# Moving loads, the place of Pool's sum, and the low parts of h at the seams of a staged two-layer kernel

## The chip, the cores and the metric

The kernel runs on one core of one Trainium2 chip. The metric is the device time of one execution in microseconds, taken as the median of several runs. Engines are named as in the profile: PE (TensorE matmul, PEld its weight loads), DVE (VectorE), ACT (ScalarE), POOL or Pool (GpSimd), SP (SyncE, which here issues the loads).

## The reference

x has shape (B, T, S) = (1024, 24, 1024), W1 (1024, 24), W2 (1024, 1024), all float32. The output is (1024, 1024).

```
h = jax.nn.sigmoid(jnp.einsum('bts,st->bs', x, W1) + b1)
return h @ W2.T + b2
```

So every h[b, s] is a sum over 24 values x[b, t, s] with the weights W1[s, t], and then h meets W2 in a plain matrix product. x is 100 MB and is read once.

## The kernel before, in words

**Stages.** The rows b are in 8 blocks j of 128, the columns s in 8 chunks c of 128. A stage takes four blocks j (512 rows) and two to four chunks. There are five, numbered 0 to 4, in `STAGES` (L19 to L25), each as (first block, first chunk, number of chunks, number of t that Pool takes, places, fate). Stages 0 and 1 are the first 512 rows with chunks 0 to 3 and 4 to 7, stages 2, 3 and 4 the other 512 rows with chunks 0 to 2, 3 to 5 and 6 to 7. "The last seam" is the one between stages 3 and 4.

**Two ways for x.** In each stage the t below `pools[i]` (4 or 6) go to Pool, the others to PE and DVE.
- PE's way: the tile of one t (an *item*: 512 rows by all columns of the stage) is loaded into one of 5 slots of `ring` (L201). For each chunk PE turns it (four 128x128 transposes into one of 6 banks `xbank`, L232), and DVE adds it, weighed, into `acc` (L354; the first t of a stage starts `acc`, L348). One chunk of one t is a *unit*, of kind "x".
- Pool's way: the tile of one t is loaded in two halves of 256 rows (*parts*, numbered m through the whole kernel) into 6 slots of `nat` (L195). Pool multiplies a part by the row of W1 (`weigh`, L485) and adds the sum of the t before (`add_sum`, L495). The sum over Pool's t is then turned by PE like an x tile and added without a weight (L352): these are the units of kind "n".

**Order of units.** `units[i]` (L50 to L56) lists the units of a stage: x of all t but the last two, then the n units, then x of t = 22 and 23. PE and DVE both walk through that list, and item_end, sum_turned and chunk_end are worked out from it. In stage 4 (two chunks, six t of Pool's) units 0 to 31 are t = 6 to 21, 32 and 33 are n, 34 and 35 are t = 22, 36 and 37 are t = 23.

**Order of loads.** SP issues everything in one order written out in the tables. At place `at` of a stage, just ahead of the item of t = pools[i] + at, it issues one part if `at` is in the places. The parts run two ahead of the stages: with 10, 12, 12, 12 and 10 places the last two of each stage's places carry parts of the next stage. Parts 44 to 55 are stage 4's; 44 and 45 are issued at places 15 and 17 of stage 3. An item waits until PE has turned the item five before it (L200); a part waits until the sum has passed on from its slot (part m on the sum of part m-4, L191) or, behind a stage's end, until PE has turned the sum (L193).

**h and the products.** When a chunk of a stage is complete, ACT takes the sigmoid (L431) and casts it to `h_hi` (L456); `h_lo` is h - h_hi. Stages 0 to 3 have h_lo from Pool: `low_parts(i - 1)` (L497 to L501) runs behind the third part of stage i. The product of a stage is done by PE during the next stage, between the units, by `product_step` (L264, matmuls at L301): h_hi times w_hi and w_lo, and h_lo times w_hi. `steps_due` (L160) says how many steps are due after each unit. For the first two outputs the steps with h_lo come behind those with h_hi of both. Outputs go through two banks `pbank`; ACT copies them to `y` (L443) or DVE adds them to `y` (L371, `add_out`), and PE waits for that before it uses a bank again. In stage 4, `REST` = 12 of the steps are held back until all its units are turned (L318 to L320).

**The tail.** ACT's sigmoid of stage 4 waits until all products of stage 3 are summed (L450), DVE makes h_hi and h_lo in 128x128 pieces (L387, L389), PE multiplies into eight banks (L332), DVE adds to y (L371), SP stores (L211).

Of the kernel before, what the change touches and what calls it, by code (L numbers as in the profile page):

```python
# [5 lines left out]
F32 = mybir.dt.float32  # L6
F32R = mybir.dt.float32r
ALU = mybir.AluOpType
# [7 lines left out]

STAGES = (  # L19
    (0, 0, 4, 4, (2, 3, 5, 7, 9, 11, 13, 15, 17, 18), "keep"),  # L20
    (0, 4, 4, 6, (0, 2, 3, 5, 6, 8, 9, 11, 12, 14, 15, 17), "last"),
    (4, 0, 3, 6, (0, 2, 3, 5, 6, 8, 9, 11, 12, 14, 15, 17), "keep"),
    (4, 3, 3, 6, (0, 2, 3, 5, 6, 8, 9, 11, 12, 14, 15, 17), "add"),
    (4, 6, 2, 6, (0, 2, 3, 5, 6, 8, 9, 11, 12, 13), "last"),
)  # L25


def rec_kernel(nc, x, W1, b1, W2, b2, out):
    B, T, S = x.shape
# [3 lines left out]
    OH = O // BANK  # L33
    NS = len(STAGES)
    LAST = NS - 1
# [7 lines left out]

    chunks = [s[2] for s in STAGES]
    pools = [s[3] for s in STAGES]
    fate = [s[5] for s in STAGES]
    NK0, NK = pools[0], max(pools)
# [2 lines left out]

    units = []
    for i in range(NS):
        order = [("x", t, c) for t in range(pools[i], T - 2) for c in range(chunks[i])]
        order += [("n", 0, c) for c in range(chunks[i])]
        order += [("x", t, c) for t in range(T - 2, T) for c in range(chunks[i])]
        units.append(order)  # L56
    first_unit = [sum(len(o) for o in units[:i]) for i in range(NS)]
    UNITS = sum(len(o) for o in units)
    first_h = [sum(chunks[:i]) for i in range(NS)]
# [11 lines left out]
    parts = [(i, k, f) for i in range(NS) for k in range(pools[i]) for f in range(2)]  # L71
# [18 lines left out]
    with ExitStack() as ctx:  # L90
# [12 lines left out]
        h = sb("h", [P, CMAX, BANK])  # L103
        h_hi = sb("h_hi", [P, CMAX, BANK], F32R)
        h_lo = sb("h_lo", [P, CMAX, BANK], F32R)
# [32 lines left out]
        h_hi_ready = sem("h_hi_ready")  # L138
        h_lo_ready = sem("h_lo_ready")
# [42 lines left out]
        def _(sp):  # L182
            sp.dma_start(w1[:, :].rearrange("p (c t) -> p c t", t=T),
                         W1.rearrange("(c p) t -> p c t", p=P)).then_inc(w1_loaded, 16)
            m = 0
            for i, (j0, c0, n, _, places, _) in enumerate(STAGES):
                for at in range(T - pools[i]):
                    if at in places:
# [3 lines left out]
                        elif m >= NATS:  # L192
                            sp.wait_ge(unit_turned, sum_turned(parts[m - NATS][0]))  # L193
                        sj, sc, sn = STAGES[s][0] + HALF * f, STAGES[s][1], STAGES[s][2]
                        sp.dma_start(nat[:, m % NATS, :, :sn * P],  # L195
# [141 lines left out]
        @block.vector  # L337
        def _(dve):
            def add_unit(i, v):
                u = first_unit[i] + v  # L340
                kind, t, c = units[i][v]
                bank, total = xbank[u % XBANKS][:, :], acc[:, c, :]
                weight = w1[:, bass.ds((STAGES[i][1] + c) * T + t, 1)]
                dve.wait_ge(unit_turned, u + 1)
                if v < chunks[i]:
                    if i > 0 and c < chunks[i - 1]:
                        dve.wait_ge(h_ready, first_h[i - 1] + c + 1)
                    nc.vector.tensor_scalar(total, bank, weight, None, ALU.mult).then_inc(unit_added, 1)  # L348
                    return
                dve.wait_ge(unit_added, u - chunks[i] + 1)  # L350
                if kind == "n":
                    nc.vector.tensor_tensor(total, bank, total, ALU.add).then_inc(unit_added, 1)  # L352
                else:
                    nc.vector.scalar_tensor_tensor(out=total, in0=bank, scalar=weight, in1=total,  # L354
                                                   op0=ALU.mult, op1=ALU.add).then_inc(unit_added, 1)

            def split_w2(m):
                n, c = divmod(m, SC)
                cols = slice(n * BANK, (n + 1) * BANK)
                dve.wait_ge(w_hi_ready, m + 1)  # L360
                nc.vector.tensor_tensor(w_lo[:, c, cols], pbank[m % 2][:, :], w_hi[:, c, cols].bitcast(F32),  # L361
                                        ALU.subtract).then_inc(w_lo_ready, 1)

            def add_out(i, n, bank):

                j, cols = out_half(n)
                dve.wait_ge(out_summed, OUTS * i + n + 1)
                dve.wait_ge(part_kept, kept_at[i])
                if i > 0 and fate[i - 1] == "add":
                    dve.wait_ge(y_added, added_at[i - 1] + n + 1)  # L370
                nc.vector.tensor_tensor(y[:, j, cols], bank[:, :], y[:, j, cols], ALU.add).then_inc(y_added, 1)  # L371

            dve.wait_ge(w1_loaded, 16)
            for i in range(NS):
                for v in range(len(units[i])):
                    add_unit(i, v)
                    if i == 0 and v - 2 in W2S:
                        split_w2(W2S[v - 2])
                    if i > 0 and fate[i - 1] != "keep" and v >= 2:
                        for n in range(outs_due(i, v - 2), outs_due(i, v - 1)):  # L380
                            add_out(i - 1, n, pbank[n % 2])

            for c in range(chunks[LAST]):
                for j in range(JT):
                    rows = slice(j * P, (j + 1) * P)
                    dve.wait_ge(h_ready, first_h[LAST] + c * JT + j + 1)
                    nc.vector.tensor_copy(h_hi[:, c, rows], h[:, c, rows]).then_inc(tail_hi, 1)  # L387
                    dve.wait_ge(tail_hi, c * JT + j + 1)
                    nc.vector.tensor_tensor(h_lo[:, c, rows], h[:, c, rows], h_hi[:, c, rows].bitcast(F32),  # L389
                                            ALU.subtract).then_inc(tail_lo, 1)  # L390
            for n in range(outs_due(LAST, len(units[LAST]) - 2), OUTS):
                add_out(LAST - 1, n, pbank[n % 2])
            for n in range(OUTS):
                add_out(LAST, n, xbank[(UNITS + n) % XBANKS] if n < XBANKS else pbank[n - XBANKS])
# [66 lines left out]
        @block.gpsimd  # L461
        def _(pool):
            nc.gpsimd.memset(ident[:, :], 0.0).then_inc(ident_zeroed, 1)
            pool.wait_ge(ident_zeroed, 1)
            nc.gpsimd.affine_select(out=ident[:, :], in_=ident[:, :], compare_op=ALU.not_equal, fill=1.0, base=0,
                                    pattern=[[-1, P]], channel_multiplier=1).then_inc(ident_ready, 1)
            nc.gpsimd.memset(b2x[:, :].bitcast(F32), 0.0).then_inc(b2_zeroed, 1)
            nc.gpsimd.memset(ones[:, :].bitcast(F32), 1.0).then_inc(ones_ready, 1)
            pool.wait_ge(ones_ready, 1)
            pool.wait_ge(b2_zeroed, 1)  # L470
            pool.wait_ge(b2_rounded, 2)
            low = b2x[32:33, :].rearrange("a (h n) -> a h n", n=BANK)
            nc.gpsimd.tensor_tensor(low, h[32:33, 0:OH, :], low.bitcast(F32), ALU.subtract).then_inc(b2_ready, 1)
            pool.wait_ge(b2_ready, 1)

            def weigh(m):

                i, k, f = parts[m]
                _, c0, n, _, _, _ = STAGES[i]
                row = w1all[:, k, c0 * P:(c0 + n) * P].unsqueeze(1).to_broadcast([P, HALF, n * P])  # L480
                slot = nat[:, m % NATS, :, :n * P]
                pool.wait_ge(nat_loaded[m % NATS], 16 * (m // NATS + 1))
                if k == 0 and f == 0 and i < 3:
                    pool.wait_ge(set_kept, (EARLY, EARLY + NK, SETN)[i])
                nc.gpsimd.tensor_tensor(slot, slot, row, ALU.mult).then_inc(nat_weighed, 1)  # L485

            def add_sum(m):

                i, k, _ = parts[m]
                n = STAGES[i][2]  # L490
                slot = nat[:, m % NATS, :, :n * P]
                pool.wait_ge(nat_weighed, m + 1)
                if k > 1:
                    pool.wait_ge(nat_added, sums_made(m - 2))
                nc.gpsimd.tensor_tensor(slot, slot, nat[:, (m - 2) % NATS, :, :n * P], ALU.add).then_inc(nat_added, 1)  # L495

            def low_parts(i):  # L497
                for c in range(chunks[i]):
                    pool.wait_ge(h_hi_ready, first_h[i] + c + 1)
                    nc.gpsimd.tensor_tensor(h_lo[:, c, :], h[:, c, :], h_hi[:, c, :].bitcast(F32),  # L500
                                            ALU.subtract).then_inc(h_lo_ready, 1)  # L501

            for m, (i, k, f) in enumerate(parts):
                weigh(m)
                if k > 0:
                    add_sum(m)
                if i > 0 and k == 1 and f == 0:
                    low_parts(i - 1)


_INS = ["r_x", "L0_rec_W1", "L0_rec_b1", "L0_rec_W2", "L0_rec_b2"]
# [18 lines left out]
```

## Time and profile before

| what | value |
|---|---|
| median of 3 runs | 311.82 us (311.63 to 311.99) |
| the profiled execution | 311.89 us, its span 310.1 us |
| mean granted TensorE clock | 0.982 |
| PE busy | 257.8 us, 83% of the span |
| PE weight loads | 220.0 us, 71% |
| DVE busy | 246.4 us, 79% |
| POOL busy | 215.2 us, 69% |
| ACT busy | 50.9 us, 16% |
| DMA | 109.48 MB, of which 104.97 MB read |
| chain that ended last | PE 51%, DMA 31%, DVE 7%, issue 5%, ACT 3% |

The span runs from the first to the last instruction of the profiled execution; 1.8 us of its time lie around it. All times below are us from the start of the span. Starts and ends of matmuls in a timeline are modelled and overlap by a fraction of a microsecond; the chain cuts them where the next begins. A wait is put down to the engine or DMA that released it last.

### The profile page before, as it was taken

The page shows a single profiled execution, that of the slowest core. Times are in us where ns is not written, and L with a number is a line of the kernel's source. Part 1 is how long each engine was busy: PE and PEld are TensorE (multiplying, and loading weights), DVE is VectorE, ACT ScalarE, POOL GpSimd, SP SyncE. Part 2 cuts the span into 40 slices and gives each one's busy share as a digit, 9 for nine tenths or more (in the row PEclk, how much of TensorE's full clock was granted, in tenths as well). Part 3 has the DMA queues.
Part 4 walks back from the last instruction along what each step waited for, and adds up shares of the span by engine and source line. Part 5 has one row for each costly group of instructions (what it writes and reads, how often), then busy time and mean ns, then how long its engine had stood idle before and what let it go on. Part 6 is the DMA issues. An engine that isn't in the chain of part 4 may idle for free.

```text
span 310.1 us, 4779 instructions
## 1 busy us (share of the span) xinstructions
PE 257.8 (83%) x1761; PEld 220.0 (71%) x1761; DVE 246.4 (79%) x368; ACT 50.9 (16%) x85; POOL 215.2 (69%) x125
## 2 busy tenths in 40 slices
PE   0947678648888999999579999937999988999894
PEld 0846677647766888889468887835888885888783
DVE  0729899829998978889977987877878898798865
ACT  4211223203253100100420000040101104000120
POOL 3119676626379999995799977479988848999000
PEclk9979999959999999999999999999999999999999
DMA  7999999999999999999999999999999999999007
GB/s 223 398 390 385 387 385 386 402 387 388 385 387 384 387 386 388 386 385 384 373 374 374 385 381 381 381 385 373 373 373 373 370 359 340 339 349 332 29 2 272
DMA packets 67675, 109.48 MB, mean 353 GB/s; under 512 B 3642, under 2 KB 40514, under 8 KB 67652
## 3 DMA queue, kind: packets, MB, share of 16 engines
q1 hardware_dynamic: 67056, 107.06, 96.8%
q10 hardware_dynamic: 596, 2.11, 1.7%
q8 instruction: 14, 0.23, 0.3%
q14 instruction: 9, 0.07, 0.1%
HBM read 104.97 MB, written 4.19 MB: 352 GB/s over the span
## 4 chain that ended last, share of the span: by engine, by line
PE 51%; DMA 31%; DVE 7%; issue 5%; ACT 3%; SPq 1%; DVEq 0%; ACTq 0%
DMA ring<-in_r_x 31%; PE xbank L232 25%; PE pbank L301 20%; DVE acc L354 4%; PE xbank L332 3%; ACT h L431 2%; DVE w_lo L361 2%; ACT h_hi L456 1%; PE pbank L291 1%; PE pbank L332 1%; PE pbank L261 0%; DVE acc L352 0%; ACT L431 0%; SPq L195 0%; SPq L201 0%
## 5 line engine op out<-in xcount | busy, mean ns | idle before, releaser
L354 DVE SCALAR_TENSOR_TENSOR acc<-xbank,w,acc 128x512 f32<-128x512 f32 x280 | 200.0, 746 | 41.1 <-PE xbank L232 35.6
L232 PE MATMUL xbank<-ident,ring 128*128 128x128 f32 x1184 | 171.5, 279 | 44.2 <-DMA ring<-in_r_x 36.0
L232 PEld LDWEIGHTS xbank<-ident,ring 128*128 128x128 f32 x1184 | 142.2, 144 | 75.7 <-issue 27.9
L485 POOL TENSOR_TENSOR nat<-nat,w1all 128x768 f32<-128x768 f32 (+2 forms) x56 | 107.2, 1916 | 60.6 <-DMA nat<-in_r_x 47.1
L495 POOL TENSOR_TENSOR nat<-nat 128x768 f32<-128x768 f32 (+2 forms) x46 | 87.8, 1908 | 3.6
L301 PE MATMUL pbank<-w_hi,h_hi 128*128 128x512 f32 x112 | 48.2, 431 | 0.3 <-ACT h_hi L456 0.2
L301 PE MATMUL pbank<-w_lo,h_hi 128*128 128x512 f32 x112 | 48.3, 432 | 0.0
L301 PE MATMUL pbank<-w_hi,h_lo 128*128 128x512 f32 x112 | 40.5, 431 | 0.0
L431 ACT ACTIVATE h<-acc,b1col 128x512 f32<-128x512 f32 (+1 forms) x22 | 12.5, 599 | 96.1 <-DVE acc L354 64.0
L443 ACT COPY y<-pbank 128x512 f32<-128x512 f32 x16 | 9.4, 587 | 79.4 <-PE pbank L301 79.4
L301 PEld LDWEIGHTS pbank<-w_hi,h_hi 128*128 128x128 f32 x112 | 21.3, 191 | 1.4 <-ACT h_hi L456 1.0
L348 DVE TENSOR_SCALAR acc<-xbank,w 128x512 f32<-128x512 f32 x16 | 11.7, 746 | 13.1 <-PE xbank L232 9.2
L301 PEld LDWEIGHTS pbank<-w_lo,h_hi 128*128 128x128 f32 x112 | 21.3, 191 | 0.6
L500 POOL TENSOR_TENSOR h_lo<-h,h_hi 128x512 fp32r<-128x512 f32 x14 | 17.7, 1282 | 2.4 <-ACT h_hi L456 2.4
L301 PEld LDWEIGHTS pbank<-w_hi,h_lo 128*128 128x128 f32 x112 | 18.4, 191 | 0.5
L413 ACT CAST w_hi<-pbank 128x512 fp32r<-128x512 f32 x16 | 9.4, 587 | 39.3 <-PE pbank L261 39.3
L371 DVE TENSOR_TENSOR y<-pbank,y 128x512 f32<-128x512 f32 x18 | 12.2, 683 | 3.0 <-PE pbank L301 3.0
L261 PE MATMUL pbank<-ident,y 128*128 128x128 f32 x64 | 10.3, 285 | 1.0 <-DVE w_lo L361 1.0
L361 DVE TENSOR_TENSOR w_lo<-pbank,w_hi 128x512 fp32r<-128x512 f32 x16 | 10.8, 678 | 0.0
L352 DVE TENSOR_TENSOR acc<-xbank,acc 128x512 f32<-128x512 f32 x16 | 10.0, 679 | 0.0
L408 ACT COPY w1all<-pbank 128x512 f32<-128x512 f32 x12 | 7.0, 587 | 18.3 <-PE pbank L250 18.3
L250 PE MATMUL pbank<-ident,w 128*128 128x128 f32 x48 | 7.7, 286 | 1.5 <-DVE w_lo L361 1.5
(37 smaller groups left out, 93.1 us busy)
## 6 DMA issues: line engine op xcount, KB each, us to landing
ring<-in_r_x SPq DMA_DIRECT2D x38, 1024.0 KB, 13.4
ring<-in_r_x SPq DMA_DIRECT2D x36, 768.0 KB, 11.1
nat<-in_r_x SPq DMA_DIRECT2D x20, 512.0 KB, 13.1
nat<-in_r_x SPq DMA_DIRECT2D x24, 384.0 KB, 11.5
ring<-in_r_x SPq DMA_DIRECT2D x18, 512.0 KB, 7.8
y<-in_L_rec_W SPq DMA_DIRECT2D x2, 2048.0 KB, 14.9
nat<-in_r_x SPq DMA_DIRECT2D x12, 256.0 KB, 8.7
out_y<-y ACTq DMA_DIRECT2D x4, 512.0 KB, 6.6
```

Of the source, the lines that this page charges most:

```text
L232: mm = pe.transpose(xbank[u % XBANKS][:, j * P:(j + 1) * P], tile, ident[:, :])
L261: mm = pe.transpose(pbank[m % 2][:, j * P:(j + 1) * P], y[:, j, c * P:(c + 1) * P], ident[:, :])
L301: mm = pe.matmul(pbank[n % 2][:, :], a[:, c, rows], w[:, STAGES[i][1] + c, cols], start=r == 0, stop=r == per - 1)
L332: mm = pe.matmul(bank[:, :], a[:, c, j * P:(j + 1) * P], w[:, STAGES[LAST][1] + c, cols], start=c == 0 and k == 0, stop=c == chunks[LAST] ...
L348: nc.vector.tensor_scalar(total, bank, weight, None, ALU.mult).then_inc(unit_added, 1)
L354: nc.vector.scalar_tensor_tensor(out=total, in0=bank, scalar=weight, in1=total, op0=ALU.mult, op1=ALU.add).then_inc(unit_added, 1)
L361: nc.vector.tensor_tensor(w_lo[:, c, cols], pbank[m % 2][:, :], w_hi[:, c, cols].bitcast(F32), ALU.subtract).then_inc(w_lo_ready, 1)
L371: nc.vector.tensor_tensor(y[:, j, cols], bank[:, :], y[:, j, cols], ALU.add).then_inc(y_added, 1)
L431: nc.scalar.activation(h[:, c, rows], acc[:, c, rows], ACT.Sigmoid, bias=b1col[:, bass.ds(STAGES[i][1] + c, 1)]).then_inc(h_ready, 1)
L485: nc.gpsimd.tensor_tensor(slot, slot, row, ALU.mult).then_inc(nat_weighed, 1)
L495: nc.gpsimd.tensor_tensor(slot, slot, nat[:, (m - 2) % NATS, :, :n * P], ALU.add).then_inc(nat_added, 1)
L500: nc.gpsimd.tensor_tensor(h_lo[:, c, :], h[:, c, :], h_hi[:, c, :].bitcast(F32), ALU.subtract).then_inc(h_lo_ready, 1)
```

## The change

It does four things.

1. Stage 3 has 10 places instead of 12 (15 and 17 are dropped), stage 4 has 12 instead of 10 (1 to 6 and 8 to 13). Parts 44 and 45 are so issued at places 1 and 2 of stage 4, part 46 at place 3, the last one still at place 13. The number of loads and their sizes stay.
2. In the last stage all x units come first and the n units last: 32, 33 are t = 22, 34, 35 are t = 23, 36, 37 are n.
3. Pool's `low_parts` is gone.
4. DVE makes the low parts of stages 0 to 3 with the same operation: chunk c of stage i-1 behind unit chunks[i] + 2c of stage i.

```diff
@@ -16,12 +16,13 @@
 
 
 
+
 STAGES = (
     (0, 0, 4, 4, (2, 3, 5, 7, 9, 11, 13, 15, 17, 18), "keep"),
     (0, 4, 4, 6, (0, 2, 3, 5, 6, 8, 9, 11, 12, 14, 15, 17), "last"),
     (4, 0, 3, 6, (0, 2, 3, 5, 6, 8, 9, 11, 12, 14, 15, 17), "keep"),
-    (4, 3, 3, 6, (0, 2, 3, 5, 6, 8, 9, 11, 12, 14, 15, 17), "add"),
-    (4, 6, 2, 6, (0, 2, 3, 5, 6, 8, 9, 11, 12, 13), "last"),
+    (4, 3, 3, 6, (0, 2, 3, 5, 6, 8, 9, 11, 12, 14), "add"),
+    (4, 6, 2, 6, (1, 2, 3, 4, 5, 6, 8, 9, 10, 11, 12, 13), "last"),
 )
 
 
@@ -50,9 +51,10 @@
 
     units = []
     for i in range(NS):
-        order = [("x", t, c) for t in range(pools[i], T - 2) for c in range(chunks[i])]
+        ahead = T - 2 if i < LAST else T
+        order = [("x", t, c) for t in range(pools[i], ahead) for c in range(chunks[i])]
         order += [("n", 0, c) for c in range(chunks[i])]
-        order += [("x", t, c) for t in range(T - 2, T) for c in range(chunks[i])]
+        order += [("x", t, c) for t in range(ahead, T) for c in range(chunks[i])]
         units.append(order)
     first_unit = [sum(len(o) for o in units[:i]) for i in range(NS)]
     UNITS = sum(len(o) for o in units)
@@ -361,6 +363,11 @@
                 nc.vector.tensor_tensor(w_lo[:, c, cols], pbank[m % 2][:, :], w_hi[:, c, cols].bitcast(F32),
                                         ALU.subtract).then_inc(w_lo_ready, 1)
 
+            def low_part(i, c):
+                dve.wait_ge(h_hi_ready, first_h[i] + c + 1)
+                nc.vector.tensor_tensor(h_lo[:, c, :], h[:, c, :], h_hi[:, c, :].bitcast(F32),
+                                        ALU.subtract).then_inc(h_lo_ready, 1)
+
             def add_out(i, n, bank):
 
                 j, cols = out_half(n)
@@ -376,6 +383,10 @@
                     add_unit(i, v)
                     if i == 0 and v - 2 in W2S:
                         split_w2(W2S[v - 2])
+
+                    c, odd = divmod(v - chunks[i], 2)
+                    if i > 0 and 0 <= c < chunks[i - 1] and odd == 0:
+                        low_part(i - 1, c)
                     if i > 0 and fate[i - 1] != "keep" and v >= 2:
                         for n in range(outs_due(i, v - 2), outs_due(i, v - 1)):
                             add_out(i - 1, n, pbank[n % 2])
@@ -494,18 +505,10 @@
                     pool.wait_ge(nat_added, sums_made(m - 2))
                 nc.gpsimd.tensor_tensor(slot, slot, nat[:, (m - 2) % NATS, :, :n * P], ALU.add).then_inc(nat_added, 1)
 
-            def low_parts(i):
-                for c in range(chunks[i]):
-                    pool.wait_ge(h_hi_ready, first_h[i] + c + 1)
-                    nc.gpsimd.tensor_tensor(h_lo[:, c, :], h[:, c, :], h_hi[:, c, :].bitcast(F32),
-                                            ALU.subtract).then_inc(h_lo_ready, 1)
-
-            for m, (i, k, f) in enumerate(parts):
+            for m, (_, k, _) in enumerate(parts):
                 weigh(m)
                 if k > 0:
                     add_sum(m)
-                if i > 0 and k == 1 and f == 0:
-                    low_parts(i - 1)
 
 
 _INS = ["r_x", "L0_rec_W1", "L0_rec_b1", "L0_rec_W2", "L0_rec_b2"]
```

## Rows read from the trace of the kernel before

**Rows 1.** The page, 40 slices of 7.75 us: DMA busy tenths and GB/s

```profile
DMA  7999999999999999999999999999999999999007
GB/s 223 398 390 385 387 385 386 402 387 388 385 387 384 387 386 388 386 385 384 373 374 374 385 381 381 381 385 373 373 373 373 370 359 340 339 349 332 29 2 272
```

**Rows 2.** Windows: length, busy time (instructions) of PE, PEld, DVE, ACT, POOL, clock, DMA share, GB/s

```profile
205.00:210.00 5.00, 1.41 (x13) 1.29 (x12) 2.91 (x5) 3.83 (x6) 4.45 (x3) 1.00 1.05 384
280.00:285.00 5.00, 5.00 (x33) 3.92 (x32) 4.29 (x7) 0.00 (x0) 4.91 (x4) 1.00 1.06 340
287.00:288.00 1.00, 1.00 (x10) 0.91 (x9) 1.00 (x2) 0.00 (x0) 0.00 (x0) 1.00 0.39 136
288.00:289.00 1.00, 1.00 (x11) 1.00 (x10) 1.00 (x3) 0.00 (x0) 0.00 (x0) 1.00 0.10 35
```

**Rows 3.** Timeline of SP in stage 4: part 55, items t = 19, 22, 23

```profile
276.10 0.37 SPq L195 DMA_DIRECT2D nat<-in_r_x  x1
276.51 0.61 SPq L201 DMA_DIRECT2D ring<-in_r_x  x1
281.86 0.37 SPq L201 DMA_DIRECT2D ring<-in_r_x  x1
283.94 0.37 SPq L201 DMA_DIRECT2D ring<-in_r_x  x1
```

**Rows 4.** DMA view of those three ring issues (276.51, 281.86, 283.94): us to landing

```profile
ring<-in_r_x SPq DMA_DIRECT2D x1, 512.0 KB, 7.7
...
ring<-in_r_x SPq DMA_DIRECT2D x1, 512.0 KB, 6.5
...
ring<-in_r_x SPq DMA_DIRECT2D x1, 512.0 KB, 5.7
```

**Rows 5.** Chain that ended last, from 240 us: start, us, what

```profile
250.64 3.07 PE xbank L232 x28
...
256.87 0.75 DVE acc L354
...
261.03 0.63 ACT h_hi L456
...
261.70 0.50 PE pbank L301
...
266.90 0.69 PE pbank L301 x3
...
282.28 0.50 PE xbank L232 x4
...
286.34 4.54 PE xbank L232 x40
290.88 2.76 PE pbank L301 x12
...
294.85 4.35 PE xbank L332 x18
```

**Rows 6.** Timeline of PE: the n units of stage 4

```profile
288.03 1.04 PE L232 MATMUL xbank<-ident,nat 128*128 128x128 f32 x8
```

**Rows 7.** Timeline of POOL: start, us, what, [idle before <- releaser]

```profile
256.12 1.27 POOL L485 TENSOR_TENSOR nat<-nat,w1all 128x512 f32<-128x512 f32 x1 [1.60 <-DMA nat<-in_r_x]
...
259.17 3.84 POOL L500 TENSOR_TENSOR h_lo<-h,h_hi 128x512 fp32r<-128x512 f32 x3 [0.41 <-ACT h_hi L456]
...
285.25 1.29 POOL L495 TENSOR_TENSOR nat<-nat 128x512 f32<-128x512 f32 x1
```

**Rows 8.** DVE by line and form, whole span: busy us, mean ns, idle before

```profile
L371 DVE TENSOR_TENSOR y<-pbank,y 128x512 f32<-128x512 f32 x18 | 12.2, 683 | 3.0 <-PE pbank L301 3.0
...
L389 DVE TENSOR_TENSOR h_lo<-h,h_hi 128x128 fp32r<-128x128 f32 x8 | 2.3, 293 | 0.3
```

**Rows 9.** Timeline of DVE around unit 6 of stage 4

```profile
265.13 0.75 DVE L354 SCALAR_TENSOR_TENSOR acc<-xbank,w,acc 128x512 f32<-128x512 f32 x1 [0.54 <-PE xbank L232]
267.17 0.69 DVE L371 TENSOR_TENSOR y<-pbank,y 128x512 f32<-128x512 f32 x1 [1.29 <-PE pbank L301]
```

## The prediction

> **What bounds the kernel now.** I read the page's slices first [rows 1]: from the second slice to the 37th the DMA engines are busy nine tenths or more, and the rate falls only where the packets get shorter (about 387 GB/s with 2 KB rows, 373 with 1.5 KB, 340 with 1 KB in the last stage). No slice in between shows a hole. So the loading of x is one long queue, and what lands last is set by the bytes ahead of it, not by their order. The short windows [rows 2] show its end: 340 GB/s in 280 to 285 us, then the share falls to 0.39 and 0.10 after 287 us.
>
> Next, when the last x loads land. SP issues the load of t=22 at 281.86 and that of t=23 at 283.94 us [rows 3]; they land 6.5 and 5.7 us after their issue [rows 4], so at 288.36 and 289.64 us. The load of t=19 is issued at 276.51 and lands 7.7 us later, at 284.2.
>
> Then the chain that ended last [rows 5]. Ahead of the last seam it passes from PE (250.64) over DVE's last unit (256.87) and ACT's cast of the third chunk (261.03) to PE at 261.70; no DMA stands in it. From 261.70 on it is PE without a gap worth naming: the first matmul with h_hi of the third chunk, transposes and products in turn, ten units of transposes in one block (286.34, 4.54 us, x40), the 12 products held back (2.76), the sigmoid, the tail's matmuls at 294.85. In the row at 282.28 a group of transposes starts a touch late (0.50 instead of 0.44 us), just where a load lands. So in the last stage PE is full and the queue is full at the same time, and the last stage ends by whichever is later.
>
> One unit in that block takes 4.54/10 = 0.454 us. It holds units 28 to 37 of the last stage. Before, 32 and 33 are Pool's sum, 34 and 35 are t=22, 36 and 37 are t=23: unit 32 starts at 288.16 (the timeline has the transposes of nat at 288.03 [rows 6], its starts lying a tenth early), unit 34 at 289.07, unit 36 at 289.98. So t=22 is there 0.71 us before PE wants it, and t=23 0.34 us before. Pool ended its last sum at 286.54 [rows 7], 1.6 us before unit 32.
>
> **Pool's halves moved behind x.** Parts 44, 45 and 46 leave the queue's places ahead of t=21, t=23 (stage 4) and t=6 of the last stage. A half is 0.26 MB, 0.77 us at 340 GB/s. So x lands 0.8 us sooner at the end of the fourth stage, up to 2.3 us sooner at t=6, and by place 10 the counts are level again (9 halves issued in both, then 10, 11, 12). From t=18 on, the bytes ahead of each load are what they were. SP has no issue more or less. What the earlier x brings: PE's start at 261.70 waits for ACT's third cast, which waits for DVE's last unit; DVE was not waiting for data there. I cost it at nothing. It removes small waits of 0.06 us like that at 282.28 (a handful, 0.3 us together), which the later loads of t=18 and t=19 take back. At least 0, at most 0.3 us gained at mid-stage, 0 at its end.
>
> **Pool's own work in the last stage.** Part 46 reached Pool at 256.12 [rows 7]. Now the queue ahead of part 44 lacks two halves and holds t=6 in their place, the same 0.5 MB, so 44 lands near 256.1; 45 and 46 follow at (0.52+0.26)/340 = 2.3 us each, 260.7. From 263.0 to 286.54 Pool ran 18 operations without a wait, 1.31 us each; ten parts from 46 on make 20, 26.2 us, and end at 286.9 (287.5 if 46 comes 0.6 late as mixed packets may make it). The three low parts (3.84 us from 259.17) that stood in between are gone, which pays for the later start. The sum is now wanted at unit 36, not before 289.98, so Pool is covered by 2.5 to 3 us. Each part's issue waits for Pool's sum four parts back: part 55, issued at 276.10 [rows 3], goes 0.3 to 1.0 us later, and t=19 queued behind it with it, to 277.5 at most. At 277.5 the data of t=17, part 54 and t=18 are still queued, so the engines do not run dry: 0 us. Without that cover it would cost up to 1 us.
>
> **The last units' order.** Now 32, 33 are t=22, 34, 35 are t=23, and 36, 37 the sum. PE wants t=22 at 288.16 and it lands at 288.36: a wait of 0.20. Two units take it to 289.27; t=23 lands at 289.64: a wait of 0.37. Then four units, not two, follow the last landing: 289.64 + 4 x 0.454 = 291.46, where it was 290.88. That is **+0.58 us** on PE, and nothing behind it gives any back: the 12 held-back products (2.76), on whose sum ACT's sigmoid waits, then the tail. DVE's four adds end before these products do, as they must only follow the transposes by one unit each; an add of the sum is not longer than a weighed one. At the upper end a restart after each wait costs another 0.07: +0.7. At the lower end the last loads land 0.4 us earlier than in this execution, and it is +0.2.
>
> **Low parts on DVE.** No row shows this operation with 512 columns on DVE. The nearest below is the tail's with 128 columns, 293 ns [rows 8]; above, the same operation on Pool, 3.84/3 = 1.28 us [rows 7]; the nearest in kind and size is DVE's y add, 683 ns [rows 8]. I take 0.68. In stages 1 to 3 of five (counting from 0), 11 of them, 7.5 us, stand behind early units of a stage, and both DVE and PE catch up at each stage's end, where they wait for the queue (205 to 210 us: PE busy 1.41, DVE 2.91 of 5 us [rows 2]). What covers them is this slack; a ring slot given back a microsecond late does not empty a queue that is issued 6 us and more ahead [rows 4]. 0, at most 0.3. In the last stage three stand behind units 2, 4 and 6. Unit 6 starts at 265.13 and the next operation on DVE is the first y add at 267.17, behind an idle 1.29 us [rows 9]: the third low part goes there, 265.8 to 266.5. PE's first use of it is the group of three products at 266.90 [rows 5], so it is 0.4 us in time: 0. Behind it on DVE stand unit 7 and the y add that frees PE's bank; were it late, both would be. At 1.28 us each the three would push each other: third done at 267.65, PE 0.75 late.
>
> The Trainium skill speaks against this part. GPSIMD Engine Reference, Key points: GpSimd shares its SBUF interfaces with VectorE and the two contend when a DVE instruction has two SBUF inputs, as h and h_hi are here. No run here shows it, since the only such operations (the tail's) run when Pool is idle.
>
> **Sum.** -0 (earlier x), 0 (Pool), +0.58 (order), 0 (low parts): the profiled execution took 311.89 us with a span of 310.1, and would become 312.47 with 310.7. The median of the runs is 311.82, 0.07 below, so I say 312.4.
>
> **Rivals.**
> *Pool and DVE contend.* For it: in the last stage Pool runs without a pause and each low part falls on one of its operations. Against: nothing measured. PE then loses 0.75 us at the third low part; since the end is the later of PE and queue, the waits for t=22 and t=23 vanish in it, and the end is +0.75 to +0.9. Where Pool too is stretched by the same time (3.8 us), part 55 and t=19 are issued near 280.5, t=19 lands at 286.2 at the earliest instead of 284.2, and it becomes +2. From 1 us of stretch on Pool this decides. 312.6 to 313.8; chance 0.17.
> *The order costs nothing,* as the last loads land 0.4 us earlier or PE gets later than them by other small delays: 311.8 to 312.0; chance 0.13.
> *The last stage moves forward.* If DVE at the end of the fourth stage did follow its data, ACT and PE start up to 1.4 us sooner; t=18 is turned sooner and t=23 issued sooner. The queue allows little: after 287 us only 0.17 MB moved [rows 2], half a microsecond's worth, yet the landing took until 289.6. Packed tightly, t=23 would land at 288.4, and the end is 288.4+1.82+2.76 = 292.98 against 293.64: -0.66, or 311.2. Against it: the chain shows no DMA at this seam, and the bytes ahead are the same. Chance 0.17, some of it for what I do not see.
> *My forecast,* +0.2 to +0.9, 312.0 to 312.7: 0.53.
>
> **Numbers.** A measurement of this kernel tells about 0.2%, 0.62 us, from no change; 312.44 is the bound above and my forecast lies on it. So its 0.53 splits into 0.26 slower and 0.27 same. Slower: 0.26 + 0.16 of contention = 0.42. Same: 0.27 + 0.13 + 0.01 = 0.41. Faster: 0.17. The range leaves out the long stretch of Pool and the last part of the faster case: 311.1 to 313.4.
>
> **What would show it.** Right: in the last stage PE waits for ring 0.2 to 0.4 us ahead of t=22 and t=23; the block of transposes ends near 291.5 with nat last; t=23 lands at 289.6 within 0.3; Pool ends near 287; from the end of the block on everything is as before, 0.6 us later; the DVE rows of h_lo say 0.68. Wrong: t=23 lands over 0.5 us earlier (the queue was not what bound), PE starts the last stage before 261.4, the h_lo rows on DVE or Pool's rows are much longer, or PE waits for h_lo or nat.

## The result, and the profile of the changed kernel

| | before | after |
|---|---|---|
| median of the interleaved runs | 311.92 us (20 runs, 311.63 to 312.42) | 313.27 us (20 runs, 312.3 to 316.13) |
| profiled execution, its span | 311.89 us, 310.1 us | 314.94 us, 313.1 us |

The ratio is 1.0052 [1.0037 to 1.0068] over all runs, so the change costs about 1.6 us (1.35 between the medians). The time lies inside the range of the forecast and moved the way it said, but its +0.58 us was too small. The times of the changed kernel spread more widely than before's, and the profiled execution lies in the upper part of that spread: it is 1.67 us above the median, so not all of its 3.05 us over before are the price of the change.

The page of the changed kernel (compare with [rows 1]; slices of 7.83 us):

```profile
span 313.1 us, 4779 instructions
...
DMA  7999999999999999999999999999999999999207
GB/s 187 398 386 389 385 387 387 402 387 388 386 386 386 388 386 379 385 384 378 345 359 378 272 384 385 387 380 378 374 373 374 373 363 347 334 342 342 69 3 268
```

Its DVE row for the low parts, by line and form (busy us, mean ns, idle before):

```profile
L368 DVE TENSOR_TENSOR h_lo<-h,h_hi 128x512 fp32r<-128x512 f32 x14 | 22.3, 1592 | 0.0
```

Two things are new. One slice in the middle (272 GB/s, 172 to 180 us) has a hole, though its busy digit is still 9; two slices ahead of it are low as well (345 and 359, where before had 373 and 374), and so is the first (187 against 223). And a low part costs DVE 1.59 us, where I had taken 0.68. Windows of the changed kernel, with the columns of [rows 2]:

```profile
170.00:175.00 5.00, 3.28 (x21) 2.57 (x20) 5.00 (x8) 0.00 (x0) 4.92 (x3) 1.00 1.01 349
175.00:180.00 5.00, 5.00 (x34) 4.26 (x33) 5.00 (x9) 0.00 (x0) 4.84 (x4) 1.00 0.95 242
```

DVE is busy the whole 10 us from 170 to 180. The timeline of SP there (start, us, what) shows that no load is issued between 168.54 and 173.74, and the rate falls behind that gap.

```profile
168.04 0.50 SPq L197 DMA_DIRECT2D nat<-in_r_x  x1
173.74 3.53 SPq L203 DMA_DIRECT2D ring<-in_r_x  x2
```

The chain that ended last, from 240 us (compare with [rows 5]):

```profile
253.24 3.07 PE xbank L234 x28
...
269.53 1.60 DVE h_lo L368
271.13 0.04 issue
271.17 0.97 PE pbank L303 x3
...
290.41 4.37 PE xbank L234 x40
294.78 2.76 PE pbank L303 x12
...
298.74 1.40 PE xbank L334 x5
```

The block of 28 transposes, 250.64 us before, starts at 253.24: in this execution 2.6 us were lost ahead of the seam, in the low slices. (How much of it the hole took is not shown: e6 below has a hole of nearly the same depth, 294 GB/s, and its block starts at 251.04, 0.4 us late.) The three products with the third chunk's low part start at 271.17 instead of 266.90, 4.27 late, directly behind DVE's h_lo. The held-back products start at 294.78 instead of 290.88 (3.90 late), the tail at 298.74 instead of 294.85 (3.89). No DMA stands in this chain behind 240 us: in this execution the last x loads were not what the last stage waited for. The waits between 262 and 276 us (us in total, times, longest) name the seam's loss:

```profile
PE pbank L303 <- DVE h_lo L368: 2.0, 1, 2.0
```

The timeline of Pool shows the other side of it. Its add takes 1.62 us while DVE makes low parts, and 1.29 us afterwards (its multiply takes 1.28 in both):

```profile
264.79 1.62 POOL L506 TENSOR_TENSOR nat<-nat 128x512 f32<-128x512 f32 x1
...
273.58 1.29 POOL L506 TENSOR_TENSOR nat<-nat 128x512 f32<-128x512 f32 x1
...
289.26 1.29 POOL L506 TENSOR_TENSOR nat<-nat 128x512 f32<-128x512 f32 x1
```

Pool's last sum ends at 290.55, against 286.54 before. Of the 3.89 us at the tail's start the last store gives back 0.8 (its 256 KB land 2.1 us after the issue, before 2.9), which leaves the 3.05 us of this execution.

### The profile page after: what moved, and what is told of

It is laid out like the page before. It is cut to its first block, busy times and chain, and to the rows that moved or that the text cites. A ratio compares the mean times of both kernels' runs of the same rounds, so it can differ in the third digit from the quotient of the medians.

```text
span 313.1 us, 4779 instructions
## 1 busy us (share of the span) xinstructions
PE 260.9 (83%) x1761; PEld 221.4 (71%) x1761; DVE 263.8 (84%) x382; ACT 50.9 (16%) x85; POOL 201.9 (64%) x111
## 4 chain that ended last, share of the span: by engine, by line
PE 53%; DMA 19%; issue 13%; DVE 10%; ACT 4%; SPq 1%; DVEq 0%; ACTq 0%
PE xbank L234 26%; PE pbank L303 22%; DMA ring<-in_r_x 19%; DVE acc L356 7%; PE xbank L334 3%; ACT h L442 2%; DVE h_lo L368 1%; DVE w_lo L363 1%; ACT h_hi L467 1%; PE pbank L293 1%; PE pbank L334 1%; PE pbank L263 1%; DVE acc L354 1%; ACT L442 0%; SPq L197 0%
## 5 line engine op out<-in xcount | busy, mean ns | idle before, releaser
L356 DVE SCALAR_TENSOR_TENSOR acc<-xbank,w,acc 128x512 f32<-128x512 f32 x280 | 197.4, 743 | 30.4 <-PE xbank L234 28.4
L234 PE MATMUL xbank<-ident,ring 128*128 128x128 f32 x1184 | 173.3, 281 | 39.6 <-DMA ring<-in_r_x 27.1
L496 POOL TENSOR_TENSOR nat<-nat,w1all 128x768 f32<-128x768 f32 (+2 forms) x56 | 108.5, 1939 | 79.5 <-DMA nat<-in_r_x 65.6
L506 POOL TENSOR_TENSOR nat<-nat 128x768 f32<-128x768 f32 (+2 forms) x46 | 90.3, 1962 | 3.6
L368 DVE TENSOR_TENSOR h_lo<-h,h_hi 128x512 fp32r<-128x512 f32 x14 | 22.3, 1592 | 0.0
L263 PEld LDWEIGHTS pbank<-ident,y 128*128 128x128 f32 x64 | 7.7, 147 | 2.2 <-DVE w_lo L363 2.1
```

The lines of the kernel that those rows point to most:

```text
L234: mm = pe.transpose(xbank[u % XBANKS][:, j * P:(j + 1) * P], tile, ident[:, :])
L263: mm = pe.transpose(pbank[m % 2][:, j * P:(j + 1) * P], y[:, j, c * P:(c + 1) * P], ident[:, :])
L368: nc.vector.tensor_tensor(h_lo[:, c, :], h[:, c, :], h_hi[:, c, :].bitcast(F32), ALU.subtract).then_inc(h_lo_ready, 1)
```

## The experiments

Ratios are to the kernel before on the same chip, with 95% intervals. There are three edits in the change: **order** (the `ahead` lines), **places** (the two lines of `STAGES`) and **low parts** (from Pool to DVE). No run has the places alone: each has the low parts of stage 3 on DVE or later on Pool. The diffs show the lines that matter and leave the rest out.

**Low parts alone.** e1 moves all of them, e2 those of stage 3's chunks (made and used in the last stage), e3 the others. Pool's own are left out where DVE has them.

```diff
+                    if i - 1 in (0, 1, 2, 3) and 0 <= c < chunks[i - 1] and odd == 0:   # e2: (3,)   e3: (0, 1, 2)
+                        low_part(i - 1, c)
```

> The kernel before with the low parts of stages 0 to 3 moved to DVE, loads and order of units as before. Contention theory (DVE and Pool slow each other while DVE reads two SBUF operands, DVE then holds PE up, ring slots come free late and the load queue runs dry): each low part takes 1.3 to 2.7 us on DVE, a slice between 145 and 185 us falls under 360 GB/s, the third low part of the last seam is late for PE by 1 to 2 us, and the time is 1.5 to 4 us over before. Queue-and-order theory (the forecast: low parts at 0.68 us hidden in DVE's slack, only the late n units cost): no change, 311.9 within 0.2.

> The kernel before with only stage 3's low parts on DVE. Contention theory: loads unharmed, PE waits 1 to 2 us for the third low part in the last stage, and as PE was full there the end moves by that: +1.5 to +2.2 us (313.4 to 314.1). Queue-and-order theory: no change, within 0.2.

> The kernel before with stages 0 to 2's low parts on DVE, stage 3's on Pool. Contention theory: DVE busy without a gap at the starts of stages 1 and 2, GB/s dips in stage 2, the last stage starts later by what the queue lost, 0 to 2.6 us, and this part is the one that differs from execution to execution: 312 to 314.5, a spread over 1 us. Queue-and-order theory: no change, within 0.2.

Measured: e1 312.27 us, 1.0020 [1.0007 to 1.0034]; e2 311.78, 1.0000 [0.9992 to 1.0009]; e3 311.94, 1.0011 [0.9997 to 1.0025]. In e1 a low part takes 1265 ns on average (683 to 1815), so contention with Pool was there without the rest of the change. Its chain shows that it does not fit into the slack at before's seam:

```profile
266.41 1.60 DVE h_lo L366
268.05 0.96 PE pbank L301 x3
...
295.69 4.36 PE xbank L332 x18
```

PE waits 1.8 us for the third low part, the three products start 1.15 us later than before's 266.90, and the tail 0.84 us later than 294.85. The last store then lands in 2.1 us instead of 2.9, so this execution has before's span of 310.1 us. In this execution the low parts alone thus make the tail 0.8 us late, and the store hides it. In e2's profile the third low part falls for the most part into a pause of Pool (266.83, 0.68 us), and PE does not wait for it. That where a low part falls among Pool's operations decides its price would explain e2's +0.00%; it is not shown. The intervals of e1 and e3 overlap.

**All but the low parts.** Places and order, the low parts left on Pool, in the last stage behind its second part:

```diff
-                if i > 0 and k == 1 and f == 0:
+                if i > 0 and (k, f) == ((1, 0) if i < LAST else (0, 1)):
```

> The changed places and the changed order of units, but all low parts on Pool; in the last stage they run behind Pool's second part instead of its third, since its third now lands after 260 us and PE wants them at 266. Queue-and-order theory: t=23 lands near 289.6 and four units follow it: +0.58 us (312.3 to 312.6), the whole of the effect. Contention theory: the same +0.2 to +0.6 at most, with the rest of the measured +1.4 absent; no dip in GB/s, Pool's operations at 1.29 us.

Measured: 313.95 us, 1.0060 [1.0046 to 1.0074]. The low parts on DVE are not needed for a loss as large as the whole change's. But Pool is later here than in the change, since it has both the later parts and the 3.84 us of low parts: part 55 is issued at 278.83, against 276.10 before [rows 3] and 277.22 and 277.33 in e10 and e11 below, which have stage 3's low parts on DVE. Windows of this kernel:

```profile
265.00:270.00 5.00, 5.00 (x34) 4.26 (x33) 3.35 (x6) 0.00 (x0) 4.84 (x5) 1.00 0.92 302
...
280.00:285.00 5.00, 4.90 (x32) 3.85 (x30) 4.20 (x7) 0.00 (x0) 4.84 (x5) 1.00 0.89 292
```

The DMA engines move 302 and 292 GB/s where before had 340 [rows 2]. The load of t=23, issued at 284.47, lands at 291.37, 1.7 us later than before. Here the "queue is full" premise breaks.

**Order alone, and its opposite.**

```diff
+        ahead = T - 2 if i < LAST else T        # e5, e9, in the kernel before
...
-        ahead = T - 2 if i < LAST else T        # e6, in the kernel after
+        ahead = T - 2
```

> The kernel before with only the order of the last stage's units changed (n last); places and low parts as before. Order theory: PE waits for t=22 and t=23 and four units follow the last landing: +0.5 to +0.7 us, loads landing as before (last 289.6). Thin-queue theory (in the last stage SP holds x loads behind parts that wait for Pool's sums; the changed places make Pool late, the loads in flight get few and GB/s falls to near 300, so the last x lands up to 1.7 us later): no fall of GB/s here, as Pool is not later, so the same +0.6 and not more.

> The order of the last stage's units alone, once more, for its trace. Order theory: t=23 lands within 0.4 us of before's 289.6, the chain goes DMA, sixteen transposes, twelve products; the tail's first matmul starts 0.5 to 1.2 us after before's 294.85; +0.25% again. No slice under 330 GB/s in the last stage and none under 370 in stage 2.

> The changed kernel with the old order of the last stage's units: places and low parts on DVE as changed. Thin-queue theory: t=23 lands 0.5 to 1.7 us later than before and PE wants it at unit 36, so +0.5 to +1.5 us; Pool's sum ends at 287 to 289 and is wanted at 288.2, another 0 to 1. Contention theory (low parts on DVE alone cost the time): as the low parts alone, +0.4 at most. Order theory: 0, all of the loss was the order.

Measured: e5 312.93 us, 1.0027 [1.0016 to 1.0037], but its profile can't be laid beside before's, so e9 repeats it: 312.80, 1.0026 [1.0017 to 1.0035], or +0.8 us. e6: 312.64, 1.0028 [1.0013 to 1.0043], 0.24% below the changed kernel's ratio; the two intervals overlap. The chain of e9 is the one forecast:

```profile
284.00 5.85 DMA ring<-in_r_x
289.85 0.14 issue
289.98 1.94 PE xbank L233 x16
291.92 2.77 PE pbank L302 x12
...
295.89 4.14 PE xbank L333 x17
```

**Pool made short.** Its multiply and add touch only the first 16 of the 256 to 512 columns of a block of rows, in the changed kernel (e7) and in the one before (e12), which leaves out most of Pool's sum.

```diff
-                nc.gpsimd.tensor_tensor(slot, slot, row, ALU.mult)
+                nc.gpsimd.tensor_tensor(slot[:, :, :16], slot[:, :, :16], row[:, :, :16], ALU.mult)
```

(and the same for its add.)

> The changed kernel with Pool's multiply and add cut to 16 of each half's columns per block row, so Pool leaves most of its sum out and is nearly idle; loads, their order and all else as changed. Low parts on DVE should then take 0.68 us each. Thin-queue theory: SP never waits for Pool, the queue stays full, last x lands near 289.6, time 312.3 to 312.6 by the order of the units alone. If what costs is in the places themselves (parts landing later), it stays at 313 or more.

> The kernel before with Pool's multiply and add cut to 16 columns per block row (most of Pool's sum is left out). A control for e7, which had the changed order and yet the time of before. If a quiet Pool gives nothing to the kernel before: 311.9, and then the order costs nothing when Pool is quiet. If it gives 0.5 to 0.9 us (loads never held behind Pool's sums): 311.0 to 311.4, and the order costs the same 0.6 to 0.9 there as in e5.

Measured: e7 311.89 us, 0.9995 [0.9987 to 1.0004]; e12 311.77, 0.9996 [0.9987 to 1.0005]. Pool's length is worth nothing before and 0.57% after, as much as the whole loss. (e7 keeps the price of the order, and the gain of the last store below cancels it.) It does not tell the two ways apart by which a long Pool can cost: by contention with the low parts, and by parts whose load is issued later. With Pool out of the way a low part costs DVE what I had estimated (e7's row by line and form):

```profile
L368 DVE TENSOR_TENSOR h_lo<-h,h_hi 128x512 fp32r<-128x512 f32 x14 | 9.7, 692 | 0.0
```

e7 still holds the order: its tail starts at 295.96, 1.1 us later than before's. It gets 0.8 back in the last store (2.1 us), which e12 does not (3.0).

**Places with stage 3's low parts on DVE.** e10 is before with places, order and stage 3's low parts on DVE; e11 the same without the order.

> The changed kernel with the low parts of stages 0 to 2 back on Pool and only stage 3's on DVE; places and order as changed. If the low parts of the first stages (DVE and Pool contending, queue running dry in stage 2 in some executions) are the part of the loss that the order does not explain: no dip near 175 us, and about the order's +0.25% (312.6), spread under 1.3 us. If it is the thin queue of the last stage: still +0.5% (313.4).

> As e10 with the old order of units too, so of the change only the places and stage 3's low parts on DVE are left. First-stages theory: 0, within 0.15%. Thin-queue theory: +0.2 to +0.4%.

Measured: e10 313.40 us, 1.0039 [1.0025 to 1.0052]; e11 313.23, 1.0040 [1.0027 to 1.0054]. e2 with the places added thus goes from +0.00% to +0.40%, and the order adds nothing on top. The traces show where it goes. The third low part takes 1.69 us in both, PE's three products with it start at 268.25 and 268.38, 1.35 and 1.48 us late, and the tails at 296.29 and 296.13, 1.44 and 1.28 late. So the delay is there at the seam, and PE is then late enough for the order to cost nothing: the last stage ends by the later of PE and the queue, not by their sum. Part of the seam's delay is a slower PE. In e10 PE reached the seam early, was busy 1.23 of the 2.5 us from 257.5 to 260, and was then granted a mean of 0.66 over the next window, part of it at the lower level of 1.2 GHz (group of four transposes 0.85 us instead of 0.44):

```profile
257.50:260.00 2.50, 1.23 (x6) 0.58 (x6) 2.25 (x5) 2.30 (x4) 1.26 (x1) 1.00 1.05 340
260.00:265.00 5.00, 4.66 (x20) 3.97 (x21) 4.27 (x6) 1.53 (x3) 4.33 (x4) 0.66 1.04 338
```

The profiles of e4, e6, e8 and e11 have the same fall, those of after and e7 have not.

**Is it the clock?** Filler: the first three units of the last stage are turned 2, 2 and 4 times, so that PE stays busy over the seam.

```diff
+                turns = (2, 2, 4)[v] if i == LAST and v < 3 else 1
-                for j in range(JT):
+                for j in [j for _ in range(turns) for j in range(JT)]:
```

> e11 (changed places, stage 3's low parts on DVE, else before; +0.40%) with PE kept busy while it waits for ACT's casts at the last seam: units 0, 1 and 2 of the last stage are turned 2, 2 and 4 times into the same bank instead of once. Clock theory (x landing early lets PE finish early, it then sits idle from 258 to 260 us, and the granted clock falls to 0.56 and 0.75 from 260 to 265 us, where PE is the bound): clock 1.00 in 260 to 265, the tail's first matmul 0.5 to 1.2 us earlier than e11's 296.1, +0.0 to +0.2%. Thin-queue theory (SP held behind Pool's parts): no gain, +0.4%.

> The changed kernel with the same filler on PE. Clock theory: most executions gain 0.5 to 1 us, median 312.3 to 312.8 instead of 313.3. If the clock is not a part of it: 313.3, or a little over, for the added transposes.

Measured: e13 (e11 with filler) 313.35 us, 1.0046 [1.0030 to 1.0062]; e14 (after with filler) 312.86, 1.0038 [1.0017 to 1.0059]. The clock stayed full:

```profile
260.00:265.00 5.00, 4.88 (x31) 3.98 (x32) 4.82 (x7) 1.20 (x2) 3.85 (x3) 1.00 1.07 339
...
275.00:280.00 5.00, 5.00 (x34) 4.25 (x33) 4.54 (x7) 0.00 (x0) 4.84 (x5) 1.00 0.89 285
```

and e13 was no faster than e11; e14's interval overlaps the changed kernel's. So no gain from the clock is shown, though the filler also takes time from PE, so the clock's own price stays open. In e13's profile the third low part took 0.68 us and PE had its products at 266.44, in time. What remains there is the rate, 285 GB/s from 275 to 280, and a wait of 1.2 us for an x load. In e14's, with all low parts on DVE, PE waits 1.7 us for the third low part and the tail starts at 296.30.

**Are x loads held behind Pool's?** SP issues in order, and parts 50 to 55 wait for Pool's sums. In e8, e17 and e18 ACT issues them instead, starting from after, e13 and e16 (e4 with filler), and SP leaves them out.

```diff
+                if i == LAST - 1:
+                    for m in range(50, len(parts)):
+                        act.wait_ge(nat_added, sums_made(m - NATS + 2))
+                        act.dma_start(nat[...], x_v[...]).then_inc(nat_loaded[m % NATS], 16)
```

> The changed kernel with the loads of parts 50 to 55 issued by ACT's queue behind the last cast of stage 3 instead of by SP, each with the same wait for Pool's sum. SP then issues the last stage's x loads as soon as PE frees a slot. Thin-queue theory: x loads from t=14 on are no longer held, the time falls from 313.3 to 312.3 to 312.7. If SP's order was not what held them: no change against the changed kernel (313.3).

> e4 (places and order as changed, low parts on Pool; +0.6%) with the filler. If the clock was the bigger part: it falls to +0.25 to +0.35%. If Pool's lateness and the x loads held behind its parts are: clock 1.00 but t=23 still lands at 291 or later and +0.5 to +0.6% stays.

> e13 (changed places, stage 3's low parts on DVE, filler; +0.46%) with parts 50 to 55 issued by ACT's queue behind its last cast of stage 3, with the same waits for Pool's sums, so that SP's x loads are not held behind them. Held-loads theory: t=20 to t=22 are issued one by one as PE frees their slots, not in a burst behind part 55; no window of the last stage under 325 GB/s, PE no wait for ring over 0.5 us, +0.0 to +0.2%. If something else of the places costs: +0.4% stays.

> e16 (places and order as changed, low parts on Pool, filler; +0.63%) with parts 50 to 55 on ACT's queue. Held-loads theory: t=23 lands near 289.6 to 290.2 instead of 291.1 and what stays is the order and what Pool's later sum costs at units 36 and 37, +0.25 to +0.45%. Otherwise +0.6% stays.

Measured: e8 312.61 us, 1.0035 [1.0013 to 1.0056], which overlaps with after, so in the changed kernel itself no price of the holding is shown. e17 313.10, 1.0035 [1.0022 to 1.0048], which overlaps with e13: inconclusive. Its profiled execution, the slowest of its six (315.16 us), goes against the expectation: 259 and 291 GB/s in 270 to 275 and 275 to 280 us with no x load behind a part, and a wait of 2.0 us for the third low part. A low rate is thus not by itself a sign of held loads: an item also waits until PE has turned the one five before it, so a late PE gives `ring` slots back late. e1, with before's places, has 302 and 312 GB/s in the same two windows. e16 314.16, 1.0063 [1.0051 to 1.0075], against e18 312.96, 1.0031 [1.0020 to 1.0042]: disjoint, 0.32% or 1.0 us for nothing but who issues six halves. In e16's timeline of SP, x loads go out in a burst (at 279.01, 279.53 and 280.08) right behind part 55:

```profile
278.60 0.37 SPq L196 DMA_DIRECT2D nat<-in_r_x  x1
```

The window 275 to 280 of e16, and then of e18:

```profile
275.00:280.00 5.00, 5.00 (x34) 4.25 (x34) 4.29 (x7) 0.00 (x0) 4.84 (x5) 1.00 0.94 314
```

```profile
275.00:280.00 5.00, 5.00 (x35) 4.26 (x34) 4.56 (x7) 0.00 (x0) 4.84 (x5) 1.00 1.10 348
```

The chain of e16, and then of e18:

```profile
283.17 7.87 DMA ring<-in_r_x
...
297.09 2.99 PE xbank L334 x12
```

```profile
283.29 6.72 DMA ring<-in_r_x
...
296.06 4.14 PE xbank L336 x17
```

The load of t=23 is issued within 0.12 us of the same time in both, but lands at 291.04 in e16 and at 290.01 in e18, and e16's tail starts 1.03 us later: the bytes ahead of it were asked for too late, and the time lost on the DMA engines did not come back. This is the price of the holding where Pool still makes the low parts (part 55 at 278.60).

**The last store.** e7 and e1 both end with a store of 2.1 us instead of 2.9. DMA view of before, from 306.7 us to the end:

```profile
q14 instruction: 1, 0.01, 0.6%
...
out_y<-y SPq DMA_DIRECT2D x1, 256.0 KB, 2.9
```

An 8 KB transfer of instructions (q14, at 307.1 us) runs in the middle of the last output. e15 is before with 28 waits that are already met, at the start of DVE's program:

```diff
+            for _ in range(28):
+                dve.wait_ge(w1_loaded, 16)
```

> The kernel before with 28 waits on a semaphore that has long come, at the start of DVE's program, where it idles for data. Instruction-fetch theory (the 8 KB instruction transfer that in the kernel before runs among the last output's packets, 2.1 us before the end, is DVE's next block; 14 more operations with their waits on DVE moved it to 9.5 us before the end, and the last store then landed in 2.1 instead of 2.9 us): the last store lands in 2.1 us, time -0.6 to -0.9 us: 311.0 to 311.3. Otherwise: 311.9.

Measured: 311.22 us, 0.9972 [0.9962 to 0.9982]. It is faster than both kernels, and nothing is left out of it. Its tail starts at 295.16, no earlier than before's, so the gain lies behind it. Its DMA view from 307 us to the end has no q14:

```profile
out_y<-y SPq DMA_DIRECT2D x1, 256.0 KB, 2.1
```

In e15, e1, e7 and the changed kernel the transfer of q14 comes ahead of the first store from SP, and all eight take 2.1 to 2.2 us. It need not fall into the last one to cost: in e2 and e10 it comes 0.5 us ahead of the issue of the last store, which still takes 2.9 and 2.8, and in e3 3.3 us ahead of it, with 2.5 to 2.6 us for all eight stores.

## Why the prediction was right or wrong

**What failed is two zeros of the sum.** It had 0 for the low parts on DVE and 0 for what the places do to Pool and the queue. Pool made short takes back 0.57% (e7), so the loss beyond the order hangs on Pool's length; the two steps below are the two ways.

**Order: right in mechanism, a little small.** "Then four units, not two, follow the last landing" is e9's chain. Forecast +0.58; the trace has the tail start 1.04 us later (295.89 against 294.85), because t=23 landed 0.16 us later than in the profile of before (289.80 against 289.64), the restart took 0.14 to 0.18 us, and sixteen transposes took 1.94 instead of 1.82 us. The runs say +0.8 us [0.5 to 1.1].

**Low parts: the first step that failed; right price, wrong company.** I had put the third one "0.4 us in time: 0". The 0.68 us forecast for a low part was 0.69 measured without Pool (e7). Beside Pool it is 1.27 (e1) to 1.59 us (after), and Pool's add goes from 1.29 to 1.62 us. In the changed kernel PE waits 2.0 us for the third low part, and its products start 4.27 us late where the stage had come 2.6 late, so 1.7 us are lost here; in e1, with nothing else changed, PE waits 1.8 us and the tail starts 0.84 us late. The rival "Pool and DVE contend", given 0.17, is what the changed kernel shows, in the place it named and inside its 312.6 to 313.8, though it had put the loss there at 0.75 us. That waiting for h_lo is also the thing I had listed under "wrong". The Trainium skill (GPSIMD Engine Reference, Key points) has the contention as a rule; the runs agree and give it a size. I had quoted the rule, and still took the row without contention. Alone, the low parts cost +0.20% net (e1), while the shorter last store gives 0.28% back (e15); if these add, they are worth about 0.48%, an estimate and no measurement.

**Places: the second step that failed.** I wrote "the engines do not run dry: 0 us. Without that cover it would cost up to 1 us." I had seen that part 55 goes later and that x queues behind it, and counted three loads still queued. In e10 and e11 part 55 is issued at 277.2 and 277.3 and the next x load at 277.6 and 277.7, about the 277.5 I had allowed, and yet the queue is not as full as its busy share says: in windows of 5 us a share of 0.89 to 0.95 and 285 to 314 GB/s in e4, e11, e13 and e16, where before had 1.06 and 340 [rows 2]. (The "t=23 (stage 4)" of that part of the prediction is stage 3's.) Pool's sum itself was in time, as forecast: it ends at 290.55 in the changed kernel's profile, and PE waits for no nat. At the last seam several parts, not one, come late, since each waits for Pool's sum. Priced by runs: 1.0 us for the holding alone, but only where the low parts stay on Pool (e16 to e18), which makes part 55 2.5 us late. Added to stage 3's low parts on DVE, the places cost 0.40% (e11 against e2); how that splits between the holding, the clock and the low part that now meets Pool's add stays open, as e17 did not separate from e13. In the changed kernel's profile PE waits for no x load in the last stage, and e8 overlaps with it, so there the holding is not shown to cost anything. And "what lands last is set by the bytes ahead of it, not by their order" holds only while every load is issued in time.

**The hole in stage 2** was in no case of mine. I had said that "a ring slot given back a microsecond late does not empty a queue". In after, e6, e8 and e14 the slice at 172 to 180 us shows 272 to 317 GB/s; in e10, whose low parts there are on Pool, 385, and in e7, with a short Pool, 385. But e1 and e3 have the low parts on DVE too, and show 381 and 383. So low parts beside Pool were in every profile that has the hole, but did not always make one. I did not settle what else it takes. Nor is it shown to be why after's times spread up to 316.1 us: the profiled executions of e6 (312.49 us) and e14 (312.51) have the hole and are not slow, and that of e17 (315.16) is slow without one.

**What hid a part of it.** The changed kernel also gains the 0.8 us of the last store, which I did not see. The parts are not additive: order 0.26% (e9), places with stage 3's low parts on DVE 0.40% (e11) and all low parts 0.20% (e1, with the store's gain in it) make 0.86%, the whole is 0.52%. Stage 3's low parts are in two of these, and the later of PE and queue decides (e10 and e11 measure the same).

## What to carry to other kernels

A busy share near one doesn't show a full queue: look at GB/s against the best rate for the same row length, and at the time from issue to landing. When a load waits for a semaphore, price everything behind it in the same issuing queue, and look in the chain whether that wait is the one that ends last. A duration taken from a row in which the neighbour is idle is a lower bound if the neighbour will be busy; where a rule says that the two contend, put the stretched duration into the sum. An experiment that measures no change can hold two that cancel, as e1 does: compare the chain too. And when edits meet in one stage whose end is the later of two chains, measure them together, as their separate prices don't add.

## What the runs showed that I had not expected

A transfer of instructions, 8 KB on a queue of its own, goes through the same DMA engines as the data. When it fell among the output stores, the last one took 2.5 to 3.0 us instead of 2.1, and 28 more instructions on DVE were enough to have it ahead of them: 0.28% less time, more than most edits of this study moved. It also means that any edit that changes the number of instructions on DVE can shift a kernel's time by 0.8 us for a reason that has nothing to do with the edit.

PE's granted clock fell at the seam in five of the kernels with the places: in e10 PE was busy 1.23 of 2.5 us, then 0.66 was granted on average over 5 us; in e4 and e11 it was at full again from 265 us on. In e17 it fell later, to 0.68 in 270 to 275 us, behind 5 us in which PE was busy 3.04. It does not follow every such pause: in e7 PE was busy 0.89 us of the same 2.5 and in e3 1.06, and the clock stayed at 1.00.
